# A mixture-of-experts stage with rows in blocks of 256 and W1 as the stationary operand

## The chip, the cores and the metric

The kernel runs on one core of one Trainium2 chip. The metric is the device time of one execution in microseconds, from the median of several runs. One execution was also taken by the profiler; all rows of the profile come from that one.

## The reference, cut to what matters

A graph layer over 3125 nodes of 256 features: a message-passing part over 50,000 edges, a linear attention, and then the part that the change touches, a mixture of 8 experts with the two best experts per node:

```
logits = xt @ Wr + br                      # xt: 3125 x 256, 8 experts
top_p, top_idx = top_k(softmax(logits), 2)
weights = top_p / top_p.sum(-1)
xe = xn * ln_g[e] + ln_b[e]                # per expert
h  = gelu(xe @ W1[e] + b1[e])              # 256 -> 1024
y  = h @ W2[e] + b2[e]                     # 1024 -> 256
out = x + sum over the two experts of weight * y
```

3125 nodes x 2 choices make 6250 rows. The reference's own routing of its inputs gives the eight experts 949, 684, 740, 736, 734, 917, 618 and 872 rows.

## The kernel before, in words

The edge part runs from the start to about 585 us, two dense layers and a batch norm follow, then the routing builds lists of rows by expert (about 660 to 696 us). Meanwhile each expert's weights have been split once into a high part (rounded to the matmul's fp32r format) and a low part (the rest) and stored in a table in memory, `split_table`, of 4 MB per expert. A product is made of three matmuls: high x high, high x low, low x high.

The expert stage works on slots of 128 rows, all of one expert (`SLOTS` = 56; `MAIN` = 52 always run, the other 4 only if the lists need them). For slot j the steps are:

- POOL `fetch(j)` (L750): copies a column of row numbers (L752) and gathers 128 token rows from the token table with an indirect DMA (L757).
- PE `slot_transpose` (L1065) turns them; DVE `slot_scale` (L1759) applies ln_g and ln_b; ACT `slot_high` (L1355) and DVE `slot_low` (L1782) make the two parts.
- PE `slot_up` (L1080): 12 matmuls with the tokens stationary and 512 columns of W1 moving; the result has rows on partitions. DVE `slot_bias` (L1768) adds b1, broadcast over partitions, ACT `slot_gelu` (L1341) follows.
- PE `slot_hidden_transpose` (L1090): 8 transposes of 128x128; ACT `slot_copy` (L1348) and DVE `slot_copy` (L1775) take the high and low parts out of PSUM.
- PE `slot_down` (L1104): 24 matmuls of 256 columns. DVE `slot_out` (L1789) adds b2 into `ys`, ACT `slot_weigh` (L1359) multiplies by the gate weight.
- POOL `put(j)` (L761): copies the row numbers (L764) and adds the 128 rows to the output with an indirect accumulating DMA (L768). Before it copies the next row numbers it waits until the put before has landed (`acc_in`).

PE's order is written out by hand: `slot_step(j)` is hidden transposes of j, up of j+1, token transposes of j+2, down of j. A hardware loop of four steps reads the expert numbers into registers at its head (`experts_of`). POOL's order is fetch(j+4), put(j), fetch(j+5), put(j+1) and so on. `tok` holds 4 slots, `ys` 4 slots.

The weights of an expert are in `wsplit`, two sets by the parity of e. SP waits until `y_b` says that all slots of expert e-2 are through, loads the two biases (L547, L548) and the 4 MB of expert e (L544), and announces them with `w_ready`. With the lists of these inputs this happens inside the stage for e = 2 to 7; the loads of experts 0 and 1 come before it.

## Time and profile before

| | |
|---|---|
| median of 3 runs (lowest, highest) | 1082.4 us (1082.07, 1085.88) |
| the profiled execution | 1084.07 us, its span 1082.2 us |
| PE busy over the span | 973.2 us, 90% |
| DVE, ACT, POOL busy | 628.0, 507.3, 574.0 us |
| expert stage, from the row lists to the end | 696 to 1082 us |
| mean granted TensorE clock | 0.971 of full speed |

The span is the time from the first to the last instruction; the execution's own time has 1.9 us around it. Busy time of PE is that of pipelined matmuls, so it counts overlaps of neighbours once. A line such as L1104 is a line of the kernel; the same line can stand for PE (the matmul) and PEld (the load of its stationary operand). "Idle before" an instruction is followed by what ended it; "issue" means that nothing which the profile shows was waited for.

### The profile page before, as it was taken

The page shows a single profiled execution, that of the slowest core. Times are in us where ns is not written, and L with a number is a line of the kernel's source. Part 1 is how long each engine was busy: PE and PEld are TensorE (multiplying, and loading weights), DVE is VectorE, ACT ScalarE, POOL GpSimd, SP SyncE. Part 2 cuts the span into 40 slices and gives each one's busy share as a digit, 9 for nine tenths or more (in the row PEclk, how much of TensorE's full clock was granted, in tenths as well). Part 3 has the DMA queues.
Part 4 walks back from the last instruction along what each step waited for, and adds up shares of the span by engine and source line. Part 5 has one row for each costly group of instructions (what it writes and reads, how often), then busy time and mean ns, then how long its engine had stood idle before and what let it go on. Part 6 is the DMA issues. An engine that isn't in the chain of part 4 may idle for free.

```text
span 1082.2 us, 18882 instructions
## 1 busy us (share of the span) xinstructions
PE 973.2 (90%) x5439; PEld 819.6 (76%) x5440; DVE 628.0 (58%) x1185; ACT 507.3 (47%) x1030; POOL 574.0 (53%) x632
## 2 busy tenths in 40 slices
PE   3898899999999999799998971599999999999995
PEld 2587788888878878687785551588888888888894
DVE  6555455555545555488884158655555555555552
ACT  3654455545445454355543445434444444444442
POOL 3377777777777777767770030124253353453442
PEclk9999999999999999899999986899999999999998
DMA  9767778787777877997752019412545626635321
GB/s 228 214 147 242 249 246 262 237 279 236 251 253 238 269 248 248 280 301 240 248 183 84 25 48 330 185 30 35 201 79 180 212 49 205 189 69 149 103 34 21
DMA packets 98047, 198.29 MB, mean 183 GB/s; under 512 B 19875, under 2 KB 52843, under 8 KB 96954
## 3 DMA queue, kind: packets, MB, share of 16 engines
q1 hardware_dynamic: 67358, 131.60, 35.1%
q0 software_dynamic: 28896, 64.46, 24.5%
q10 hardware_dynamic: 1724, 1.42, 0.6%
q8 instruction: 31, 0.51, 0.2%
q14 instruction: 38, 0.31, 0.1%
HBM read 147.86 MB, written 49.97 MB: 183 GB/s over the span
## 4 chain that ended last, share of the span: by engine, by line
PE 64%; POOL 14%; DVE 7%; issue 7%; DMA 5%; ACT 1%; SPq 0%; DVEq 0%; POOLq 0%; ACTq 0%
POOL work L715 14%; PE banks L1104 13%; PE banks L1080 13%; PE banks L451 10%; PE banks L439 9%; PE banks L1090 4%; PE banks L428 2%; PE banks L979 2%; PE banks L989 2%; PE banks L918 2%; DMA work<-node_table,srcT 2%; PE banks L863 2%; DMA work<-token_table,tokc 1%; DMA xs<-in_x 1%; PE banks L1065 1%
## 5 line engine op out<-in xcount | busy, mean ns | idle before, releaser
L715 POOL DMA_INDIRECT work<-node_table,srcT x396 | 397.4, 1003 | 160.1 <-issue 117.7
L487 DVE TENSOR_TENSOR work<-banks,work 128x512 f32<-128x512 f32 x198 | 128.9, 682 | 117.4 <-DMA work<-node_table,srcT 114.4
L451 PE MATMUL banks<-work 128*128 128x256 f32 x792 | 186.5, 386 | 9.1 <-issue 8.5
L439 PE MATMUL banks<-w_edge,eaT 128*128 128x256 f32 x792 | 182.9, 380 | 3.0 <-DVE work L487 3.0
L451 PEld LDWEIGHTS banks<-work 128*128 128x128 f32 x792 | 152.0, 193 | 33.8 <-issue 13.0
L439 PEld LDWEIGHTS banks<-w_edge,eaT 128*128 128x128 f32 x792 | 144.9, 190 | 21.5 <-DVE work L487 4.6
L1104 PE MATMUL banks<-wsplit,hidT_hi 128*128 x832 | 155.9, 288 | 1.7 <-DVE hidT_lo L1775 1.7
L1080 PE MATMUL banks<-wsplit,xeT_hi 128*128 x416 | 134.8, 405 | 2.7 <-DVE xeT_lo L1782 2.7
L475 ACT ACTIVATE work<-work 128x512 f32<-128x512 f32 x198 | 113.7, 626 | 39.9 <-DVE work L487 39.9
L768 POOL DMA_INDIRECT out<-work,rowc x52 | 83.7, 1609 | 90.3 <-ACT work L1359 59.6
L1104 PEld LDWEIGHTS banks<-wsplit,hidT_hi 128*128 128x128 f32 x832 | 129.2, 191 | 2.1 <-issue 1.9
L464 ACT COPY wts<-banks 128x256 f32<-128x256 f32 x66 | 24.6, 373 | 217.4 <-PE banks L451 217.4
L1104 PE MATMUL banks<-wsplit,hidT_lo 128*128 x416 | 117.7, 283 | 0.0
L1341 ACT ACTIVATE work<-work 128x512 f32<-128x512 f32 x104 | 65.7, 632 | 101.6 <-DVE work L1768 101.6
L1775 DVE TENSOR_TENSOR hidT_lo<-banks,hidT_hi 128x512 fp32r<-128x512 f32 x104 | 67.0, 686 | 63.6 <-ACT hidT_hi L1348 63.5
L1080 PEld LDWEIGHTS banks<-wsplit,xeT_hi 128*128 128x128 f32 x416 | 75.1, 191 | 16.8 <-issue 3.4
L1768 DVE TENSOR_TENSOR work<-banks,wts 128x512 f32<-128x512 f32 x104 | 71.5, 688 | 21.4 <-PE banks L1080 19.9
L1080 PE MATMUL banks<-wsplit,xeT_lo 128*128 x208 | 82.3, 396 | 0.0
L1104 PEld LDWEIGHTS banks<-wsplit,hidT_lo 128*128 128x128 f32 x416 | 79.6, 191 | 0.0
L757 POOL DMA_INDIRECT work<-token_table,tokc x52 | 52.6, 1012 | 45.9 <-POOL tokc L752 40.7
L1359 ACT ACTIVATE work<-work,slot_f 128x256 f32<-128x256 f32 x52 | 26.5, 509 | 100.7 <-DVE work L1789 100.7
L1090 PE MATMUL banks<-ident,work 128*128 128x128 f32 x416 | 54.7, 274 | 10.9 <-issue 10.0
(226 smaller groups left out, 1414.5 us busy)
## 6 DMA issues: line engine op xcount, KB each, us to landing
wsplit<-split_table SPq DMA_DIRECT2D x8, 4096.0 KB, 14.7
work<-in_edge_attr SPq DMA_DIRECT2D x65, 384.0 KB
wts<-in_L_ffn_W SPq DMA_DIRECT2D x64, 256.0 KB, 5.0
split_table<-raw_hi SPq DMA_DIRECT2D x64, 256.0 KB, 2.6
split_table<-raw_lo SPq DMA_DIRECT2D x64, 256.0 KB, 4.4
work<-node_table,srcT POOLq DMA_INDIRECT x396, 5.1
xs<-in_x SPq DMA_DIRECT2D x8, 560.0 KB
wts<-in_L_ffn_b SPq DMA_DIRECT2D x8, 512.0 KB, 3.8
```

The source lines that it names most:

```text
L439: last = nc.tensor.matmul(b[:, k * DIM:(k + 1) * DIM], eaT[:, u, 2 * q + k], w_edge[:], start=True, stop=True)
L451: last = nc.tensor.matmul(bank[5][:, 0:DIM], onehot[:, u, j], msg[:, u, j], start=(j == 0), stop=(j == GT - 1))
L475: nc.scalar.activation(msg[:, u, 2 * q:2 * q + 2], msg[:, u, 2 * q:2 * q + 2], ACT.Relu).then_inc(msg_ready, 1)
L487: nc.vector.tensor_tensor(msg[:, u, 2 * q:2 * q + 2], bank[2 + q][:].rearrange("p (k c) -> p k c", k=2), xg[b][:, 2 * q:2 * q + 2], ALU.ad ...
L715: pool.indirect_dma_start(out=xg[n % NB][0:rows, j], out_offset=None, in_=node_table, in_offset=bass.IndirectOffsetOnAxis(ap=srcT[0:rows, ...
L768: pool.indirect_dma_start(out=out, out_offset=bass.IndirectOffsetOnAxis(ap=rowc[:, u:u + 1], axis=0), in_=ys[:, b], in_offset=None, bounds ...
L1080: last = nc.tensor.matmul(bank[1 + c][:], x[:, u, k], w, start=(k == 0 and m == 0), stop=(k == 1 and m == 2))
L1090: last = nc.tensor.transpose(bank[3 + c][:, k * P:(k + 1) * P], hid[:, u, (4 * c + k) * P:(4 * c + k + 1) * P], ident[:])
L1104: last = nc.tensor.matmul(bank[5][:, 0:DIM], x[:, k], w_set[:, lo:lo + DIM], start=(k == 0 and m == 0), stop=(k == HIDDEN // P - 1 and m = ...
L1341: nc.scalar.activation(s, s, ACT.Gelu).then_inc(hid_g, 1)
L1768: nc.vector.tensor_tensor(hid[:, u, c * 512:(c + 1) * 512], bank[1 + c][:], b1, ALU.add).then_inc(hid_b, 1)
L1775: nc.vector.tensor_tensor(hidT_lo[:, 4 * c:4 * c + 4], bank[3 + c][:].rearrange("p (k c) -> p k c", k=4), hidT_hi[:, 4 * c:4 * c + 4].bitc ...
```

## The change

The expert stage works on blocks of 256 rows of one expert (`BLOCKS` = 32, `MAIN` = 28 always run). The diff, cut to its core:

```
+ROWS = 2 * P
+BLOCKS = (2 * NODES + EXPERTS * (ROWS - 1)) // ROWS
+SLOTS = 2 * BLOCKS
-MAIN = SLOTS - 4
+MAIN = BLOCKS - 4
...
+        w1_hi = nc.alloc_sbuf_tensor_at("w1_hi", [P, HALVES, HIDDEN], F32R, ...)
+        w1_lo = nc.alloc_sbuf_tensor_at("w1_lo", [P, HALVES, HIDDEN], F32R, ...)
...
         def load_biases(sp, e):
-            sp.dma_start(bias[:, e % 2, 0:HIDDEN], a["L0_ffn_b1"][e].partition_broadcast(P))...
-            sp.dma_start(bias[:, e % 2, HIDDEN:HIDDEN + DIM], a["L0_ffn_b2"][e].partition_broadcast(P))...
+            sp.dma_start(bias[:, e % 2], a["L0_ffn_b2"][e].partition_broadcast(P))...
```

PE: W1 is the stationary operand, so the hidden rows come out transposed already; the hidden transposes go away.

```
+            def up(i, u, fresh):
+                pe.wait_ge(xeT_low, i + 1)
+                for m in range(MS):                       # MS = 8 pieces of 128 hidden columns
+                    if m % 2 == 0:
+                        pe.wait_ge(w1_high, MS // 2 * i + m // 2 + 1)
+                        pe.wait_ge(w1_low, MS // 2 * i + m // 2 + 1)
+                        if not fresh:
+                            pe.wait_ge(hid_g, MS * (i - 1) + m + 2)
+                    for k in range(HALVES):
+                        for n, (x, w) in enumerate(((xeT_hi, w1_hi), (xeT_lo, w1_hi), (xeT_hi, w1_lo))):
+                            last = nc.tensor.matmul(bank[1 + m // 2][:, m % 2 * ROWS:(m % 2 + 1) * ROWS],
+                                                    w[:, k, m * P:(m + 1) * P], x[:, u, k], ...)
+                    if m % 2 == 1:
+                        last.then_inc(hid_ps, 1)
...
+            def down(i, u, e, fresh):
+                for m in range(2):
+                    if not fresh:
+                        pe.wait_ge(y_b, 2 * i + m - 1)
+                    for k in range(MS):                   # 24 matmuls of 256 columns into bank 5 + m
...
+            def block_step(i, u, tu, r, e_here, fresh=False):
+                up(i + 1, 1 - u, False)
+                turn(i + 2, tu, r, False)                 # 4 token transposes
+                down(i, u, e_here, fresh)
```

ACT: bias and gelu in one instruction, straight out of PSUM, and the low part of W1 copied to its fixed buffer. `b1T` is filled once, by a transpose and a copy before the stage.

```
+            def block_gelu(i, u, e, e_next, fresh):
+                for b in range(MS // 2):
+                    act.wait_ge(hid_ps, MS // 2 * i + b + 1)
...
+                    for m in (2 * b, 2 * b + 1):
+                        nc.scalar.activation(hid[:, m], bank[1 + b][:, ...], ACT.Gelu,
+                                             bias=b1T[:, bass.ds(e, 1), m]).then_inc(hid_g, 1)
+                    act.wait_ge(hid_g, MS * i + 2 * b + 2)
+                    nc.scalar.copy(hidT_hi[:, u, 2 * b:2 * b + 2], hid[:, 2 * b:2 * b + 2])...
+                    if e_next is not None:
+                        weights_low(i + 1, b, e_next, False)
```

`weights_low` (ACT) and `weights_high` (DVE) copy one of four pieces, 128x512, of the low and high W1 of block i's expert from `wsplit` to `w1_lo` and `w1_hi`; at the first piece they wait for `w_ready`, and for each piece until `up` of the block before has read it. DVE's order in the loop for block i is, for b = 0 to 3, `weights_high(i + 2, b)` and `hidden_low(i + 1, b)` (with `block_scale(i + 2)` before the last pair), then `block_low(i + 2)` and `block_out(i)` for both halves.

POOL: a block is fetched and put in two halves of 128 rows, as pairs.

```
+            def fetch(i, r, u, fresh):
+                pool.wait_ge(tok_in[u], 32 * r)
+                if not fresh:
+                    pool.wait_ge(tok_T, i - TOKS + 1)
+                for m in range(2):
+                    nc.gpsimd.tensor_copy(tokc[...], tok_i[:, bass.ds(2 * i + m, 1)]).then_inc(cur_ready, 1)
+                    pool.wait_ge(cur_ready, 2 * i + m + 1)
+                    pool.indirect_dma_start(out=tok[:, 2 * u + m], ...).then_inc(tok_in[u], 16)
+            def put(i, u, fresh=False):
+                for m in range(2):
+                    if not fresh or m == 1:
+                        pool.wait_ge(acc_in, 16 * (2 * i + m))
+                    nc.gpsimd.tensor_copy(rowc[:, m:m + 1], row_i[:, bass.ds(2 * i + m, 1)]).then_inc(row_ready, 1)
+                    pool.wait_ge(row_ready, 2 * i + m + 1)
+                    pool.wait_ge(y_w, 2 * i + m + 1)
+                    pool.indirect_dma_start(out=out, ..., in_=ys[:, 2 * u + m], compute_op=ALU.add).then_inc(acc_in, 16)
...
+            fetch(AHEAD, 0, AHEAD, True)                  # AHEAD = 3; blocks 0 to 2 are fetched before
+            put(0, 0, True)
+            with pool.Fori(0, (MAIN - 4) // TOKS) as t:
+                for k in range(TOKS):
+                    fetch(TOKS * (t + 1) + k, t + 1, k, False)
+                    put(TOKS * t + 1 + k, (1 + k) % 2)
```

`tok` holds 4 blocks, `ys` 2 blocks (4 halves); `hidT_hi` and `hidT_lo` are doubled. The routing rounds each expert's rows up to 256 instead of 128.

## Rows read from the trace of the kernel before

**Rows 1.** The page's first line.
```profile
span 1082.2 us, 18882 instructions
```

**Rows 2.** Windows: stretch, its us, busy PE, PEld, DVE, ACT, POOL, clock, DMA share, GB/s.
```profile
699.00:715.00 16.00, 11.91 (x56) 9.54 (x57) 7.14 (x15) 4.71 (x9) 4.61 (x8) 0.79 0.12 34
715.00:765.00 50.00, 48.86 (x336) 44.60 (x335) 29.14 (x58) 22.09 (x42) 21.12 (x28) 1.00 0.23 38
...
990.80:1060.00 69.20, 67.80 (x463) 61.77 (x462) 40.89 (x80) 31.63 (x60) 27.93 (x36) 1.00 0.38 103
```

**Rows 3.** Timeline of PE: one slot, and the head of the next loop.
```profile
848.85 1.04 PE L1090 MATMUL banks<-ident,work 128*128 128x128 f32 x8
849.64 0.70 PE L1080 MATMUL banks<-wsplit,xeT_hi 128*128 x2
...
852.62 0.48 PE L1104 MATMUL banks<-wsplit,hidT_hi 128*128 x2
...
856.47 1.09 PE L1090 MATMUL banks<-ident,work 128*128 128x128 f32 x8 [0.73 <-issue]
```

**Rows 4.** Timeline of POOL: two first fetches, put then fetch, fetch then put.
```profile
696.68 1.03 POOL L757 DMA_INDIRECT work<-token_table,tokc  x1 [0.83 <-POOL tokc L752]
...
698.71 1.00 POOL L757 DMA_INDIRECT work<-token_table,tokc  x1 [0.80 <-POOL tokc L752]
...
830.31 1.61 POOL L768 DMA_INDIRECT out<-work,rowc  x1 [0.93 <-POOL rowc L764]
...
833.00 1.01 POOL L757 DMA_INDIRECT work<-token_table,tokc  x1 [0.88 <-PE banks L1065]
...
870.35 1.01 POOL L757 DMA_INDIRECT work<-token_table,tokc  x1 [0.89 <-POOL tokc L752]
...
872.50 1.61 POOL L768 DMA_INDIRECT out<-work,rowc  x1 [0.94 <-POOL rowc L764]
```

**Rows 5.** Timeline of SP and POOL at the first and last of six loads.
```profile
766.04 0.43 SPq L544 DMA_DIRECT2D wsplit<-split_table  x1
...
766.68 1.61 POOL L768 DMA_INDIRECT out<-work,rowc  x1 [2.60 <-ACT work L1359]
...
781.98 0.18 POOL L764 COPY rowc<-row_i 128x1 int32 x1 [11.58 <-DMA out<-work,rowc]
783.10 1.61 POOL L768 DMA_INDIRECT out<-work,rowc  x1 [0.94 <-POOL rowc L764]
...
991.62 0.43 SPq L544 DMA_DIRECT2D wsplit<-split_table  x1
...
1006.66 0.18 POOL L764 COPY rowc<-row_i 128x1 int32 x1 [10.67 <-DMA out<-work,rowc]
```

**Rows 6.** Issue to landing of a put (L768), a fetch (L757), a load (L544).
```profile
DMA to landing us min/median/max: 3.7/3.8/15.3
...
DMA to landing us min/median/max: 2.7/2.8/12.7
...
DMA to landing us min/median/max: 13.4/14.7/15.8
```

**Rows 7.** Waits of PE in the stage: total us, times, longest.
```profile
PE banks L1065 <- DMA work<-token_table,tokc: 5.6, 2, 4.9
```

**Rows 8.** Chain that ended last, in time: first up, first down; the last put.
```profile
702.32 4.73 PE banks L1080 x12
...
713.03 2.87 PE banks L1104 x24
...
1073.54 1.57 POOL L768 DMA_INDIRECT out<-work,rowc  x1 [1.73 <-ACT work L1359]
```

**Rows 9.** Groups by line: busy us, mean ns, idle before.
```profile
L1274 ACT ACTIVATE work<-banks,cvec 128x448 f32<-128x448 f32 x14 | 8.9, 634 | 14.8 <-PE banks L979 14.8
...
L534 ACT CAST raw_hi<-wts 128x512 fp32r<-128x512 f32 x64 | 38.7, 604 | 0.0
...
L1775 DVE TENSOR_TENSOR hidT_lo<-banks,hidT_hi 128x512 fp32r<-128x512 f32 x104 | 67.0, 686 | 63.6 <-ACT hidT_hi L1348 63.5
```

More of the change, by code:

```diff
@@ L1058, in _, with turn @@
             pe.wait_ge(lists_ready, 1)
[L1060 to L1061 removed]
+            def turn(i, tu, r, fresh):
+                pe.wait_ge(tok_in[tu], 32 * (r + 1))
                 if not fresh:
[L1063 to L1066 removed]
@@ L1791, in slots, with weights_high @@
-            def slots(j0, n):
-                fresh, end, e = j0 == 0, j0 + n, {}
-                def experts(j, m):
-                    e.update(zip(range(j, j + m), experts_of(DVE, j, m)))
-                experts(j0, 3)
+            def weights_high(i, b, e, fresh):
+                if b == 0:
+                    dve.wait_ge(w_ready, e + 1)
+                if not fresh:
+                    dve.wait_ge(hid_ps, MS // 2 * (i - 1) + b + 1)
+                piece = slice(2 * b * P, 2 * (b + 1) * P)
+                w_set = wsplit[:, bass.ds(e % 2, 1), 0:HALVES * HIDDEN].rearrange("p a (k c) -> p (a k) c", k=HALVES)
+                nc.vector.tensor_copy(w1_hi[:, :, piece], w_set[:, :, piece].bitcast(F32)).then_inc(w1_high, 1)
@@ L1815, in _ @@
-            slots(0, MAIN)
+                        for b in range(MS // 2):
+                            weights_high(i0 + 1, b, e[i0 + 1], False)
+                            hidden_low(i0, 0, b)
+                for i in range(i0, end):
+                    u = (i - i0) % 2
+                    for b in range(MS // 2):
+                        if b == MS // 2 - 1 and i + 2 < end:
+                            block_scale(i + 2, u, e[i + 2], False)
+                        if i + 2 < end:
+                            weights_high(i + 2, b, e[i + 2], False)
+                        if i + 1 < end:
+                            hidden_low(i + 1, 1 - u, b)
+                    if i + 2 < end:
+                        block_low(i + 2, u, False)
+                    block_out(i, u, e[i])
+                    if u == 0 and i + 3 < end:
+                        experts(i + 3, min(2, end - i - 3))
```

376 lines of the change are left out of this document (166 added, 210 removed).

## The prediction

> **What bounds the kernel now.** I read the page first, then the trace by stretches. The span is 1082.2 us [rows 1]; the profiled execution took 1084.07, the median of the runs is 1082.4, so I count on the span and carry its end over almost one to one (0.2 us). The change touches only the expert stage, from the token lists at 696 us to the end, 386 us. There PE is busy for nearly the whole of each stretch at full clock, DVE and ACT for about half [rows 2]. One slot of PE [rows 3]: 8 hidden transposes in 0.79 us (848.85 to 849.64), up with 2 token transposes in 2.98 (to 852.62; up alone some 2.85), down of 24 matmuls in 2.87, 0.120 each [rows 8]. With the change-overs 6.73 us a slot, and each loop of four begins late by 0.93 us (down ends at 855.5, the next transposes start at 856.47). 52 slots x 6.73 + 12 x 0.93 = 361 us: PE sets the time, and little else is idle on its path.
>
> But POOL is not far behind, and this decides the case. A put costs: issue, landing 3.8 us later [rows 6], then the row copy and the next issue after 1.12 (a row copy at 781.98, the put at 783.10 [rows 5]), so 4.9 to 5.1 us between puts against 6.73 a slot. When SP loads an expert's 4 MB, the put issued some 0.65 us later lands only with the load's end: load 766.04, put 766.68, next row copy 781.98 after 11.58 us of idle; at the last, load 991.62, row copy 1006.66 [rows 5]. That is so in all six such loads (15.9, 15.1, 15.9, 16.2, 14.6, 15.0 us from load to row copy; mean 15.45), and the maxima of put and fetch landing, 15.3 and 12.7 us, say the same [rows 6]. POOL loses about 11.3 us each time and wins it back in the 6 to 8 slots that follow, because a slot leaves it 1.6 us. PE noticed it once, by 0.7 us (of the two waits for tokens, 5.6 us, the other 4.9 is the start) [rows 7].
>
> **The change, part by part.** The router gives 949, 684, 740, 736, 734, 917, 618 and 872 rows: 52 slots of 128 now, 27 blocks of 256 then. MAIN is 28, so 28 blocks run, one of them empty: 56 slots' worth of down and token transposes where there were 52.
>
> *PE per block.* Up becomes 48 matmuls of 256 columns with a 128-column weight load each, the shape and pitch of down, 0.120 us: 5.76 (two slots' up now: 5.7). Down: 48 x 0.120 = 5.76. Four token transposes: 0.45. Hidden transposes: none (2 x 0.79 saved). 12.0 us a block, against 13.46 for two slots.
>
> *Start.* Two fetches instead of one before the first transposes: +2.03 [rows 4]. Scale, high and low double in width: up(0) starts at 705.2 instead of 702.3 [rows 8]. Up(0) lasted 4.73 [rows 8] against 2.85, since PE came out of idle (the granted clock is 0.79 in that stretch, part of it at 1.2 GHz, and 1.00 afterwards [rows 2]): +1.9, so it ends at 712.9. Up(1) needs xeT_low(1), which DVE and ACT reach only after four gelu pieces of about 1.92 us behind the first hid_ps (707.9): 715.7, plus scale 1.0, high 0.6, low 0.7: 718.3. Again 1.9 for the clock after the idle: up(1) ends 726.0, down(0) ends 732.2. (Before, down(0) ended at 715.9.)
>
> *PE alone to the end.* 26 x 12.0 + 5.76 for the last down + 7 loop heads x 0.93 = 324.3: 1056.5. The last put: the final two downs are 5.76 apart but four puts are a chain of 4.92 each, so the last issue is at about 1064.8 and the end 8.66 later, as now (1073.54 to 1082.2) [rows 8]: 1073.4. So even with all else hidden the gain is 8.8 us.
>
> *ACT.* Per piece of 512: two gelus with a bias pointer (at most 0.634, the row for 448 columns out of PSUM; about 0.48 each by width), one copy to hidT_hi and one to w1_lo at 0.604 [rows 9]. Without any overlap 2.2, with the 0.1 by which neighbours overlap 1.92; four pieces 7.7 to 8.9, then high 0.6 and DVE's low 0.69. From the start of up(i+1) to xeT_low(i+2): 1.6 + 7.7..8.9 + 1.3 = 10.6 to 11.8, below the 12.0 of PE. Hidden, by 0.2 to 1.4 us; if that cover were gone, each 0.1 over in a piece would cost 0.4 x 28 = 11 us.
>
> *DVE.* Four w1_hi copies, four hidden lows, two scales, one low, two outs: 13 operations of at most 0.69 [rows 9] = 9.0 of 12. Hidden. The removed bias adds and the b1 DMA of 512 KB lay off the path: nothing. The extra small constant load, b1's transpose and its copy: under 0.5 us, once.
>
> *The fixed W1 buffer.* Its copies need w_ready one step before up does. A load lands 14.7 (13.4 to 15.8) us after issue [rows 6]; SP issues it about 0.45 after y_b. After three-block experts w_ready comes 2.3 us after DVE first wants it (at 0.9 after ACT does), within the slack above: 0 us, up to 2 x 5 = 10 at worst where POOL does not hide it. Behind DVE's wait stand the hidden lows of block i+1, which down wants some 9 us later, and behind ACT's the next gelu. SP's queue is one DMA shorter per expert (0.4 us, counted in the 0.45).
>
> *POOL.* This is the term that I put the prediction on. fetch(i+3) and put(i) are now pairs: the put of m=1 waits for the landing of m=0 with no fetch in between to use the time. A block costs POOL, from the put of m=0: 3.8 landing + 1.12; to the first fetch 2.69 (830.31 to 833.00); second fetch 2.12 (2.03 at the start, 696.68 to 698.71, plus some 0.1 for register addresses); row copy and issue 2.14 (870.35 to 872.50) [rows 4]: 11.9 us. Two slots cost it 10.2. PE's mean is 12.0 + 0.93/4 = 12.2. POOL now keeps pace, but wins back only 0.3 us a block where it loses about 8 at each load, three blocks apart. Six loads happen, after blocks 3, 6, 9, 12, 15 and 19. Who waits for POOL: fetch(i+4) lies behind put(i), and turn(i+4) stands on PE in front of down(i+2). With no lag its tokens are there 12.5 us after put(i,0), 6 us before PE asks. That is all the slack.
>
> I worked the sequence, block by block: D(i), end of down(i), is the later of D(i-1) + 12.0 (+ 0.93) and tokens(i+2) + 6.3; put(i,0) is the later of POOL's chain and D(i) - 0.7; a DMA in flight during a load lands 15.45 after the load's issue at D(i) + 1.1. The intervals put(i,0) to put(i+1,0) at the six loads come out as 18.4, 20.2, 17.1, 19.7, 23.1 and 20.0, thus 6.5, 8.3, 5.2, 7.8, 11.2 and 8.1 over 11.9: 47.1. PE stalls 10.8 (block 7), 0.5, 9.9 (13), 6.6 (17) and 10.8 (20). Sum over POOL: first put 731.5; 24 x 11.87 = 284.9; three last blocks without fetches 29.5; last pair 4.9; end 8.7; holds 47.1; idle waiting for PE's results 5.4: **1112**.
>
> Two bounds of it. Whether a put issued 1.8 us before the load is held too no row shows (all six were issued after it). Held: 1126. Not held, which I take: 1112. The Trainium skill (DMA: Bandwidth & Descriptors, Queues, rings and completion order) says that a completion increment lands only after every earlier write of that DMA engine, across queues; the long landings of the trace (15.3 against 3.8) agree, and by that rule a put ahead of the load isn't held, which would be the 1112. And the chain of 11.9 rests on pitches of single fetches; with 0.05 us more at each of four steps the same sequence gives 1120, with 0.4 us less a block 1099.
>
> **Rivals.**
> 1. *POOL stays hidden; PE sets the end.* 1073.6 us, by the sum above. For it: nearly all POOL waits of today cost PE nothing. Against it: a hold of 11.3 us must fit into 6 us of slack that refills at 0.3 a block. It decides if the hold falls below some 1 us a load, or if fetches run 2 us a block faster.
> 2. *POOL is slowed further by the new copies.* DVE's four w1_hi copies are the first SBUF to SBUF copies of the stage beside POOL's issues of 1.01 and 1.61 us [rows 4, 5]. If two of the four issues of a block each wait 0.3 us (a copy lasts at most 0.69), a block costs 0.6 more than 11.9; POOL then is slower than PE at every block, not just at loads: 1059.6 + 47 + 24 x 0.6 + 5 = about 1126; range 1120 to 1140. No row shows such a wait, since no such copy is there now. The Trainium skill (SBUF — State Buffer, Two separate sides, the "DVE blocks DMA" trap) states that a fp32 SBUF to SBUF tensor_copy on DVE shuts GpSimd out of descriptor writing while it runs, which speaks against this change and would give this rival's time; no run here shows it yet.
> 3. *In between:* holds of 2 to 5 us at a load, since the load now starts in another phase of POOL's loop, and slack for the first: 1080 to 1095.
> 4. *ACT or the early w_ready sets the pace* (piece over 2.3 us): +11 to +22 on 1073.6, 1085 to 1096, hidden where POOL is slower still.
>
> **How the numbers follow.** Forecast, POOL's chain with its holds (1095 to 1120): 0.50. Rival 2 with the held put (1120 to 1145): 0.18. Rival 1: 0.20. Rivals 3 and 4: 0.12. The likeliest is 1112; its own range is 1099 to 1126. Both signs hold much of the chance, so the range runs from 1074 (half of rival 1 left out) to 1134. What a measurement tells from no change is 0.5%, 5.4 us (the three runs spread over 3.8). Faster than 1077: 0.19; within 1077 to 1087.8: 0.07; slower: 0.74.
>
> **What would show it.** Right: per-block PE work of 12.0 us with up and down at 0.120 a matmul; PE idle of 5 to 11 us at token transposes, put down to the DMA of tok, after most of the six loads; POOL's idle time at rowc on the landing of puts grown; PE's busy share down although its work fell. Rival 1: PE gaps only at loop heads, last down near 1056. Rival 2: tokc copies or DMA_INDIRECT spans on POOL longer than 0.78, 1.01 and 1.61, ending with DVE copies. Wrong would be: up at another pitch than 0.120, or POOL's block much off 11.9.

## The result, and the profile after

The changed kernel takes 1133.85 us (median of 4 runs, 1132.44 to 1138.32) against 1084.14 (4 runs, 1082.07 to 1085.88): a ratio of 1.048, 95% interval 1.0457 to 1.0503. It is slower, by 49.7 us; the forecast of 1112 us lay 29.6 above the 1082.4 that it started from. Its profiled execution took 1134.73 us, span 1133.0.

The page's first line and its line of busy times:
```profile
span 1133.0 us, 19323 instructions
PE 970.8 (86%) x5848; PEld 845.7 (75%) x5849; DVE 598.0 (53%) x1134; ACT 600.9 (53%) x1251; POOL 598.9 (53%) x648
```

The windows, with the columns of [rows 2]: a stretch from just after one load to the end of the next, one without a load, 18 us around the start of a load (issued at 864.63), the first 17 us of the last load (issued at 1015.34), and, last, 8 us in which PE works again behind the first load's wait:
```profile
790.00:835.00 45.00, 31.18 (x225) 30.98 (x226) 17.44 (x34) 23.93 (x50) 18.58 (x24) 0.81 0.44 130
835.00:862.00 27.00, 26.51 (x220) 26.12 (x219) 12.44 (x25) 17.48 (x37) 13.42 (x17) 1.00 0.22 36
862.00:880.00 18.00, 8.00 (x63) 7.61 (x63) 5.13 (x10) 9.36 (x20) 5.93 (x7) 0.86 0.77 269
1015.00:1032.00 17.00, 6.67 (x51) 6.48 (x50) 3.35 (x7) 8.12 (x17) 4.55 (x5) 0.80 0.84 285
797.00:805.00 8.00, 7.35 (x41) 7.35 (x42) 2.96 (x6) 1.13 (x2) 3.71 (x4) 0.61 0.15 17
```
Without a load PE is busy for 98% of the stretch, at full clock, as in [rows 2]. While a load moves its bytes (DMA share 0.77 and 0.84) PE is busy for 8.0 of 18 and 6.7 of 17 us, and ACT and DVE, which work on its results, have gaps too.

Who waits for whom (us in total, times, longest):
```profile
POOL rowc L773 <- DMA out<-work,rowc: 124.2, 31, 13.4
PE banks L1077 <- DMA work<-token_table,tokc: 52.6, 8, 10.3
DVE work L1774 <- PE banks L1077: 42.1, 7, 9.7
```
PE's line is that of [rows 7], grown from 5.6 us to 52.6; 45.5 us of it, in 7 waits, lie behind the start. Six of the seven are long (5.3 to 10.3 us), one for each load, as the prediction said. POOL's wait for landings of puts has grown from 85.7 us (47 times, longest 11.8) in the kernel before to 124.2. PE's token transposes wait for tokens, and DVE for PE. DVE's W1 copies wait for the signal that the weights are there once, for 4.2 us.

The timeline of SP and POOL at the first of the six loads, to be read beside [rows 5]:
```profile
772.47 0.43 SPq L552 DMA_DIRECT2D wsplit<-split_table  x1
...
773.26 1.63 POOL L777 DMA_INDIRECT out<-work,rowc  x1 [0.93 <-ACT work L1367]
788.32 0.37 POOL L773 COPY rowc<-row_i 128x1 int32 x1 [13.43 <-DMA out<-work,rowc]
789.62 1.69 POOL L777 DMA_INDIRECT out<-work,rowc  x1 [0.93 <-POOL rowc L773]
790.72 1.03 POOL L762 COPY tokc<-tok_i 128x1 int32 x1
792.59 1.04 POOL L765 DMA_INDIRECT work<-token_table,tokc  x1 [0.84 <-POOL tokc L762]
```
The first put of the block is issued 0.79 us behind the load, and the row copy that waits for its landing starts 15.85 us after the load's issue. Only then can POOL put the other half and fetch the next tokens (792.59). PE finds them missing soon after. The chain that ended last goes through the same place at each load. From 749 us, shortly behind the start, to the last load it stays on POOL and its DMAs; only behind that load (from 1030.55) does it run over PE to the end. Three of its pieces (start, us, what), and a down and an up for comparison:
```profile
728.98 5.77 PE banks L1107 x48
...
822.23 12.37 DMA out<-work,rowc
...
855.90 3.89 DMA out<-work,rowc
868.95 12.17 DMA out<-work,rowc
...
1064.32 5.76 PE banks L1091 x48
```
A put lands in 3.9 us without a load (855.90) and holds the chain for 12.2 to 14.9 us with one (at the last load it is a fetch, 12.7 us). In the page's shares of the chain, landings of puts are 11% of the span.

### The profile page after: what moved, and what is told of

It is laid out like the page before. It is cut to its first block, busy times and chain, and to the rows that moved or that the text cites. A ratio compares the mean times of both kernels' runs of the same rounds, so it can differ in the third digit from the quotient of the medians.

```text
span 1133.0 us, 19323 instructions
## 1 busy us (share of the span) xinstructions
PE 970.8 (86%) x5848; PEld 845.7 (75%) x5849; DVE 598.0 (53%) x1134; ACT 600.9 (53%) x1251; POOL 598.9 (53%) x648
## 3 DMA queue, kind: packets, MB, share of 16 engines
q0 software_dynamic: 29664, 64.98, 23.6%
## 4 chain that ended last, share of the span: by engine, by line
PE 34%; POOL 24%; DMA 16%; issue 14%; DVE 7%; ACT 3%; POOLq 1%; ACTq 1%; DVEq 0%; SPq 0%
POOL work L722 17%; DMA out<-work,rowc 11%; PE banks L459 7%; PE banks L447 6%; PE banks L1107 4%; PE banks L1091 4%; POOL work L765 3%; DMA work<-node_table,srcT 3%; PE banks L987 2%; PE banks L997 2%; PE banks L926 2%; PE banks L436 2%; POOL out L777 2%; DMA work<-token_table,tokc 1%; POOL tokc L762 1%
## 5 line engine op out<-in xcount | busy, mean ns | idle before, releaser
L1107 PEld LDWEIGHTS banks<-wsplit,hidT_hi 128*128 128x128 f32 x896 | 149.5, 205 | 0.0
L483 ACT ACTIVATE work<-work 128x512 f32<-128x512 f32 x198 | 115.2, 627 | 57.1 <-DVE work L495 56.7
L1091 PE MATMUL banks<-xeT_hi,w_hi 128*128 128x256 f32 x448 | 129.8, 290 | 11.3 <-DVE xeT_lo L1781 10.3
L1091 PE MATMUL banks<-xeT_lo,w_hi 128*128 128x256 f32 x448 | 128.3, 286 | 0.0
L1091 PE MATMUL banks<-xeT_hi,w_lo 128*128 128x256 f32 x448 | 128.2, 286 | 0.0
L1796 DVE TENSOR_TENSOR hidT_lo<-work,hidT_hi 128x512 fp32r<-128x512 f32 x112 | 77.8, 694 | 86.1 <-ACT hidT_hi L1353 86.0
L1350 ACT ACTIVATE work<-banks,b1T 128x256 f32<-128x256 f32 x224 | 93.5, 468 | 34.2 <-PE banks L1091 34.2
L1091 PEld LDWEIGHTS banks<-xeT_hi,w_hi 128*128 128x128 f32 x448 | 87.6, 195 | 13.8 <-DVE xeT_lo L1781 8.6
L1091 PEld LDWEIGHTS banks<-xeT_lo,w_hi 128*128 128x128 f32 x448 | 87.6, 196 | 0.0
L1091 PEld LDWEIGHTS banks<-xeT_hi,w_lo 128*128 128x128 f32 x448 | 87.5, 195 | 0.0
## 6 DMA issues: line engine op xcount, KB each, us to landing
wsplit<-split_table SPq DMA_DIRECT2D x8, 4096.0 KB, 15.2
```

The source lines that it names most:

```text
L483: nc.scalar.activation(msg[:, u, 2 * q:2 * q + 2], msg[:, u, 2 * q:2 * q + 2], ACT.Relu).then_inc(msg_ready, 1)
L1091: last = nc.tensor.matmul(bank[1 + m // 2][:, m % 2 * ROWS:(m % 2 + 1) * ROWS], w[:, k, m * P:(m + 1) * P], x[:, u, k], start=(k == 0 and ...
L1107: last = nc.tensor.matmul(bank[5 + m][:, 0:DIM], x[:, u, k, m * P:(m + 1) * P], w_set[:, lo:lo + DIM], start=(k == 0 and n == 0), stop=(k ...
L1350: nc.scalar.activation(hid[:, m], bank[1 + b][:, m % 2 * ROWS:(m % 2 + 1) * ROWS], ACT.Gelu, bias=b1T[:, bass.ds(e, 1), m]).then_inc(hid_g, 1)
L1796: nc.vector.tensor_tensor(hidT_lo[:, u, 2 * b:2 * b + 2], hid[:, 2 * b:2 * b + 2], hidT_hi[:, u, 2 * b:2 * b + 2].bitcast(F32), ALU.subtra ...
```

## The experiments

Lengths are compared over the expert stage: from the first copy of token numbers on POOL to the end of the span. It is 386.6 us before (the copy ahead of the first fetch of [rows 4] is at 695.6) and 435.4 in the changed kernel (697.6 to 1133.0). The reason for this measure: on the chip that ran all but the last three experiments, the part ahead of the stage took 100 to 130 us longer in every kernel, e7's version of the kernel before included. A control, e12, is the changed kernel on that chip: its stage is 438.6 us. So e1 to e11 are to be read against 438.6 as much as against 435.4. Each stage length comes from one profiled execution. "Interval" is from the first put of a block to the first put of the next; PE's waits for tokens are those behind the start.

**First group: the fetch order, the loads, the new DVE work.**

*e1: the tokens fetched one block earlier.*
```
-            for k in range(AHEAD):          # AHEAD = 3
+            for k in range(TOKS):           # TOKS = 4
                 fetch(k, 0, k, True)
...
-                    put(TOKS * t + 1 + k, (1 + k) % 2)
+                    put(TOKS * t + k, k % 2)
```


> The changed kernel with one thing else: POOL's order is fetch(i+4), put(i) instead of fetch(i+3), put(i); pairs stay pairs. My theory (PE waits for tokens because fetches stand behind puts that a weight load holds): the tokens come one block, 12 us, earlier, so the slack before PE waits grows from 6 to 18 us. The waits of PE for tokens fall from 52.6 us to under 15, the profile's span from 1133 to 1085 to 1100. Rival A (the copies of W1 and the low parts slow everything by taking ports, the order of POOL's work does not matter): 1125 to 1135. Rival B (POOL's throughput alone is the bound, whatever the order): no more than 12 us saved, 1118 to 1125.

Measured: stage 444.2 us, longer than the changed kernel's on either chip. PE's waits for tokens fell only to 36.4 us, and a new wait stands beside them. Waits of e1, and DVE at one load (issued 988.34):
```profile
DVE work L1807 <- POOL rowc L773: 63.3, 11, 7.0
PE banks L1078 <- DMA work<-token_table,tokc: 36.4, 5, 8.6
```
```profile
988.25 1.63 POOL L777 DMA_INDIRECT out<-work,rowc  x1 [0.94 <-ACT work L1368]
1004.04 0.18 POOL L773 COPY rowc<-row_i 128x1 int32 x1 [14.16 <-DMA out<-work,rowc]
...
1011.20 0.42 DVE L1807 TENSOR_TENSOR work<-banks,wts 128x256 f32<-128x256 f32 x1 [6.33 <-POOL rowc L773]
```
The theory missed, and so did both rivals. In the changed kernel POOL lags at five of the six loads: the put that is held starts 1.9 to 5.0 us behind the load's issue, at four of them behind one or two fetches, and that time isn't idle. In e1 both fetches are issued ahead of every load and the held put starts with it (at five of six loads within 0.1 us): POOL idles 13.2 to 14.2 us each time instead of 10.4 to 13.4, and the interval at a load rose from 21.4 us (mean) to 22.8 to 24.9. PE runs on for a while on its reserve of tokens, until all four results (two blocks) wait for their puts and DVE can't empty PE's banks. The reserve only moves PE's wait; POOL's throughput is the limit, at 12.3 us a block with nothing to win back.

*e2: the same, and POOL's order in a block is fetch, put, fetch, put.*
```
+                    for m in range(2):
+                        fetch(TOKS * (t + 1) + k, t + 1, k, False, (m,))
+                        put(TOKS * t + k, k % 2, False, (m,))
```


> As the run before, and the halves interleaved: fetch(i+4, half 0), put(i, half 0), fetch(i+4, half 1), put(i, half 1), so that a fetch again fills the landing time of a put. My theory: POOL needs some 10.9 us a block instead of 12.6, below PE's 12.2, and recovers from each hold before the next: PE-bound, span 1074 to 1082, waits of PE for tokens under 8 us. Rival A (ports): 1120 to 1135. Rival B (POOL's throughput alone): 24 x 1.7 = 41 us saved, 1092.

Measured: stage 402.3 us, 33.1 less than the changed kernel (36.3 less than e12); PE's waits for tokens 21.2 us in 5. Each single fetch now fills the landing of a put. POOL can take a block in some 10.6 us (the shortest intervals) and wins back a part of what a load costs; at the loads the intervals are still 18.6 to 22.7, and the theory's PE-bound stage is not reached.

*e3: small loads from the third expert on.*
```
-            sp.dma_start(wsplit[:, e % 2].bitcast(F32), split_table[e])
+            sp.dma_start(wsplit[:, e % 2, 0:64].bitcast(F32), split_table[e, :, 0:64])     # e >= 2
```


> The changed kernel, its POOL order untouched, but the weight loads of experts 2 to 7 bring 64 columns (32 KB) instead of 8192 (4 MB); those experts compute with the weights of experts 0 and 1. My theory (holds during loads are the main loss; the six intervals with a load are 8.8 us longer than the others): no holds, span 1078 to 1088. If the paired chain of 12.6 us a block were the loss and not the holds: 1110 to 1125. If ports were: 1120 to 1133.

Measured: stage 384.6 us, 50.8 less than the changed kernel and 54.0 less than e12, on the same chip. PE's waits for tokens are 3.6 us in 2, the longest of POOL's waits for a landing is 4.0 us, and the intervals between the start and the last blocks are 12.0 to 13.6. This edit leaves POOL's order alone and takes only the bytes away, so it is the load's traffic that costs these 51 to 54 us.

*e4: DVE's W1 copies reduced to 2 of 256 columns.*
```
-                piece = slice(2 * b * P, 2 * (b + 1) * P)
+                piece = slice(2 * b * P, 2 * b * P + 2)      # all but the first block
```


> The changed kernel, but from the second block on DVE copies 2 columns of each W1 high piece instead of 256 (the high part of W1 stays that of expert 0 in all other columns). My theory gives these copies (0.42 us each) a share of the 0.7 us by which POOL's block is longer than forecast: POOL issues next to them are stretched by up to 0.4 us, 0.1 to 0.3 us a block, so span 1123 to 1131. The rival that they take POOL's port for most of the loss: 1110 or less. If they cost nothing: 1132 to 1134.

Measured: stage 435.5 us, as in the changed kernel and 3.1 under e12; POOL's intervals without a load are 12.54 us, in e12 12.68. So the copies cost 0 to 3 us: the rival is out, and the theory's small share can't be told from nothing.

*e5: DVE's subtraction for the hidden low part reduced to 2 of 256 rows.*
```
-                nc.vector.tensor_tensor(hidT_lo[:, u, 2 * b:2 * b + 2], hid[:, 2 * b:2 * b + 2], ...
+                n = ROWS if i < 2 else 2
+                nc.vector.tensor_tensor(hidT_lo[:, u, 2 * b:2 * b + 2, 0:n], hid[:, 2 * b:2 * b + 2, 0:n], ...
```


> The changed kernel, but from the third block on DVE's subtraction for hidT_lo works on 2 of 256 rows (the low part of the hidden rows is left out). It is the stage's one frequent DVE instruction that reads two SBUF tensors, 0.69 us; before the change its like read PSUM. In the trace after, 10 of the 12 row copies of POOL that last 0.37 to 0.72 us instead of 0.19 lie over such an instruction, 9 of these end within 0.05 us of it. Theory (POOL's copies are held by it): row copies back to 0.19 and the expert stage (from the first copy of token numbers to the end, 435.4 us in the changed kernel) 4 to 10 us shorter, 425 to 431. Rival (coincidence): copies stay as long and the stage is 434 to 436. Only stages are compared, as the edge part on another chip may take another time.

Measured: stage 437.4 us, no gain (1.2 under e12). The reason for trying it was in the changed kernel's timelines of POOL and DVE:
```profile
1011.38 0.71 POOL L773 COPY rowc<-row_i 128x1 int32 x1 [2.41 <-DMA out<-work,rowc]
...
1011.36 0.69 DVE L1796 TENSOR_TENSOR hidT_lo<-work,hidT_hi 128x512 fp32r<-128x512 f32 x1
```
A row copy of POOL that usually lasts 0.19 us lasts 0.71 and ends with DVE's subtraction. In the changed kernel 12 of the 56 row copies last over 0.3 us, 4.0 us more in all; with the small subtraction 7 of them, 1.6 us more. The wait is real, but 2.4 us of it, spread over 28 blocks, didn't show in the stage.

The subtraction isn't the only holder, and row copies aren't all that is held. Of the 12 long row copies 3 end with a W1 copy, of e5's 7 it is 5; that of 788.32 above ends 0.04 us behind one. Puts stretch as well: one that starts while DVE is in a subtraction or a W1 copy lasts until 1.5 us after the end of that instruction.
```profile
788.22 0.43 DVE L1790 CAST w_hi<-wsplit 128x512 fp32r x1 [4.23 <-SPq L664]
...
948.41 0.42 DVE L1790 CAST w_hi<-wsplit 128x512 fp32r x1
948.46 1.87 POOL L777 DMA_INDIRECT out<-work,rowc  x1 [0.93 <-POOL rowc L773]
```
12 of the 56 puts last over 1.7 us instead of 1.6, 3 of them by a W1 copy; in the kernel before it is 1 of 52, and in e4, with the W1 copies small, 8, none by a W1 copy. All of it together is some 8 us of POOL's time in the changed kernel. No run takes both DVE instructions away.

**Second group: what a load in parts does.**

*e6: the load in eight parts of 512 KB, two on their way at a time.*
```
+            for q in range(PARTS):                                   # 8
+                s, base = ((w_in[e % 2], 0), (x_in[e % 2], 32))[q % 2]
+                if q >= 2:
+                    sp.wait_ge(s, base + 16 * (PARTS // 2 * (e // 2) + q // 2))
+                sp.dma_start(wsplit[:, e % 2, q * n:(q + 1) * n].bitcast(F32), ...).then_inc(s, 16)
```


> The changed kernel, each expert's 4 MB loaded by eight DMAs of 512 KB of which never more than two are under way. Theory (a put or fetch lands only after all that was queued before it in the DMA engines): a hold is at most about 1 MB of transfer, 3 to 4 us instead of 9 to 15, but two or three puts and fetches meet the load; the stage goes from 435.4 to 400 to 415 us. Rival (a put waits until no load is under way at all): stage 430 to 440, the longest wait of the row copy still 12 to 14 us. Second rival (SP's waits stretch the load so that the W1 copies come late): row copy waits short, but PE waits on w1_high or xeT_lo, stage over 415.

Measured: stage 416.9 us, so the second rival was right. The longest hold fell from 13.4 to 6.7 us, PE's waits for tokens to 11.5 in 9. But the load now takes longer (its parts are issued over 16.8 us), and its signal comes too late for the W1 copies, for which the fixed buffer makes DVE and ACT ask a step before PE does. Waits of e6:
```profile
POOL rowc L781 <- DMA out<-work,rowc: 100.9, 34, 6.7
DVE w_hi L1798 <- SPq L672: 43.1, 5, 10.4
PE banks L1099 <- DVE xeT_lo L1789: 28.1, 9, 6.0
```

*e7: the same edit of the load on the kernel before.*

> The kernel before with the same loads in parts. It lets POOL win back each hold already, so theory: 0 to 1 us, ratio 0.998 to 1.001, the longest wait of POOL's row copy down from 11.8 to under 5 us. If the holds cost the old kernel time that the waits don't show: ratio below 0.995.

Measured: ratio 1.0046 (1.0001 to 1.0092), stage 386.1 us against 386.6. The longest wait of POOL for a landing is 4.5 us instead of 11.8, and that buys nothing (the time is, if anything, 0.5% longer): the kernel before had the holds too, and POOL won them back.

*e8: e2 and e6 together.*

> The changed kernel with fetches one block earlier, halves interleaved and loads in parts. Theory: POOL needs 10.6 us a block (measured with the interleaved order), wins back 1.6 a block and meets no hold over 4 us: PE sets the time with 12.2 us a block; stage 377 to 386 us, ratio to the kernel before 0.990 to 0.999. Rival (lower throughput of POOL still bounds it): stage 390 to 400, ratio 1.003 to 1.012.

Measured: ratio 1.0315 (1.027 to 1.0361), stage 421.7 us, longer than e2's 402.3 and above both forecasts. Behind the start PE never waits for tokens. What PE waits for is the weights' signal, through DVE and ACT:
```profile
DVE w_hi L1802 <- SPq L672: 55.3, 5, 11.5
ACT w_lo L1354 <- SPq L672: 37.5, 5, 8.7
```
The cure of the one wait became the other: with no hold left, five of the six loads stop the copies of W1, up to 11.5 us each.

**Third group: the order alone, the floor, W1 first, and a control.**

*e9: the interleaved order without the earlier fetch.*
```
-                    fetch(TOKS * (t + 1) + k, t + 1, k, False)
-                    put(TOKS * t + 1 + k, (1 + k) % 2)
+                    for m in range(2):
+                        fetch(TOKS * (t + 1) + k, t + 1, k, False, (m,))
+                        put(TOKS * t + 1 + k, (1 + k) % 2, False, (m,))
```


> POOL's order in a block goes from fetch, fetch, put, put to fetch, put, fetch, put; the tokens are fetched at the same block as in the changed kernel, so this is one half of the edit that gave a stage of 402.3 us (the changed kernel: 435.4). Theory (the two fetches, 4.2 us, then stand behind the landings of the puts instead of between them and the next one, so POOL's block falls from 12.6 us to about 10.6, and the held landing costs as before): intervals of 10.6 to 12.2 us without a load, since PE's 12.0 now sets them; stage 400 to 412 us. Rival (the fetch one block earlier did it, by giving PE more in reserve against each hold): the intervals stay at 12.5 and the stage at 425 to 435.

Measured: stage 449.1 us, the longest of all; both sides missed. PE's waits for tokens are 57.1 us in 13, and they occur at blocks without a load too (intervals 13.2 to 15.6). POOL between two loads, and POOL's two largest waits:
```profile
958.88 1.60 POOL L778 DMA_INDIRECT out<-work,rowc  x1 [3.27 <-ACT work L1369]
...
961.52 1.18 POOL L766 DMA_INDIRECT work<-token_table,tokc  x1 [0.84 <-POOL tokc L763]
```
```profile
POOL out L778 <- ACT work L1369: 101.6, 28, 21.4
POOL rowc L774 <- DMA out<-work,rowc: 74.9, 20, 11.8
```
POOL waits 3.27 us for the result of the block's first half before it may put it, and the fetch of the second half stands behind. With tokens only three blocks ahead, PE then waits for POOL's fetch and POOL for PE's result, in turn.

*e10: interleaved order, earlier fetch, small loads.*

> The interleaved order with the earlier fetch, and from the third expert on only 64 of each partition's 8192 columns of weights are loaded (the rest of the wide copy keeps the weights of the expert before; all else is done as before). It puts the holds and POOL's block aside together and shows what PE alone would give. Theory (PE is then the bound, 12.0 us a block, 32 blocks): stage 374 to 380 us, below the 384.6 of the run with small loads alone and below the 386.6 of the kernel before. Rival (a block costs more than PE's matmuls even without holds and with POOL at 10.6 us: DVE or ACT, or POOL's own throughput): stage at or above 384.

Measured: stage 376.0 us, no wait of PE for tokens behind the start. This is what PE alone gives; 28 blocks ran, not the 32 that the expectation names. The window between start and tail, at full clock, busy for 98%:
```profile
855.00:1150.00 295.00, 290.27 (x2408) 288.09 (x2407) 157.69 (x315) 221.08 (x461) 161.50 (x188) 1.00 0.26 44
```

*e11: interleaved order, earlier fetch, and W1's parts of the load first, with their own signal.*
```
+                c = (0, 1, 4, 5, 2, 3, 6, 7)[q]            # W1 high, W1 low, W2 high, W2 low
...
+                    sp.wait_ge(w1_high, done * 2)           # the last copies of W1 of expert e - 2
+                    sp.wait_ge(w1_low, done * 2)
+                load_weights(sp, e, 0)
+                weights_there(e, 0)                         # w_ready = 2e + 1: DVE and ACT may copy W1
                 sp.wait_ge(y_b, done)
                 load_biases(sp, e)
+                load_weights(sp, e, 1)
+                weights_there(e, 1)                         # w_ready = 2e + 2: PE may start down
```


> The interleaved order with the earlier fetch, and each load in eight parts of 512 KB, two on their way at a time: first the four of W1, which start when the last copies of W1 of the expert two before are made (about a block before its last result), and which have their own signal; then, after that expert's last result, the four of W2, for which PE waits at the second layer. Theory (holds of the put's landing by whole loads cost about 50 us, and once the loads are in parts what is left is that the signal for W1 comes late, 57.0 us of waits in the run with all three edits): both gone, no wait of DVE for the weights above 3 us, longest wait of POOL for a put's landing under 7 us, stage 376 to 386 us, so the whole is 0.99 to 1.00 of the kernel before. Rival (the time that the bytes take on the queues lands on the puts however they are cut): stage above 395 us, ratio above 1.01.

Measured: stage 378.6 us, ratio 0.9975 (0.9922 to 1.0028). Of the waits for the weights' signal two are left, 2.5 us together; the longest wait for a landing is 4.5 us. The first put came 39.6 us into the stage, in e10 37.2.

*e12: the changed kernel once more, on the chip of the experiments so far.*

> The changed kernel itself on this chip, where the part before the experts takes longer. Theory and rivals agree, if the stage can be compared between chips: stage 433 to 438 us, the four last intervals with a load 20 to 23.6 us. If it is off by more than 4 us, the stage lengths of the other runs have to be read against this one instead.

Measured: stage 438.6 us, 3.2 more than on the first chip. Differences of 3 us between stages say nothing; those used here are 8 us and more, or come with their intervals.

**Fourth group: the order and the loads taken apart.**

*e13: W1 first alone, POOL's queue as in the changed kernel.*

> The changed kernel with only its loads of weights changed: parts of 512 KB, two on their way, W1's first and on their own signal. POOL's queue is that of the changed kernel (fetch, fetch, put, put, tokens three blocks ahead). Theory (the whole loads carry nearly all of the loss, POOL's order only the 8.6 us between the runs with small loads, 384.6 and 376.0): stage 386 to 394 us, intervals without a load 12.5 us, PE's waits for tokens under 5 us in all. Rival (without the reserve of the earlier fetch every part that holds a put by 3 to 7 us reaches PE, as in the run with the load in parts alone, 416.9): stage 400 to 415.

Measured: stage 410.0 us; the rival was right. PE waits for tokens 18.6 us in 8, none of them over 4.1, and POOL for landings 95.5 us, none over 5.7. POOL can't win back even small holds in its paired order.

*e14: e11, with the parts of the first two experts issued without waits between them.*
```
-                if q >= 2:
+                if q >= 2 and e >= 2:
```


> The version of the last table (parts, W1 first, interleaved order, earlier fetch), with the parts of the first two experts issued without waits between them, so that SP is not held ahead of the stage and the second load is over when the first tokens are fetched. Theory: first put 37.2 us after the token lists instead of 39.6, stage 375 to 378 us, ratio to the kernel before 0.990 to 0.996. Rival (the first put came late for another reason): first put and stage as they were, 39.6 and 378.6.

Measured: 1072.91 us (6 runs, 1071.47 to 1074.87) against 1085.38 (11 runs) of the kernel before on that chip: ratio 0.9892 (0.9859 to 0.9925), stage 375.7 us, first put at +37.0. The theory held; this version is 1.1% faster than the kernel before. The window of the steady part, and SP and POOL at a load:
```profile
740.00:1050.00 310.00, 305.43 (x2533) 303.22 (x2532) 165.43 (x327) 230.56 (x481) 161.66 (x194) 1.00 0.49 124
```
```profile
807.74 17.92 SPq L558 DMA_DIRECT2D wsplit<-split_table  x8
...
807.38 1.74 POOL L796 DMA_INDIRECT out<-work,rowc  x1 [1.56 <-ACT work L1390]
...
815.53 0.25 POOL L792 COPY rowc<-row_i 128x1 int32 x1 [3.49 <-DMA out<-work,rowc]
816.72 1.60 POOL L796 DMA_INDIRECT out<-work,rowc  x1 [0.94 <-POOL rowc L792]
```
The hold that was 13.43 us of idle is 3.49 here, and 4.9 at most in the run. PE is busy for 98.5% of 310 us with all loads inside, at clock 1.00. (The view joins the four parts of W2 and the four of the next expert's W1 into one row of eight.) The chain that ended last is PE's own; the same down recurs every four blocks:
```profile
775.84 5.77 PE banks L1130 x48
...
825.02 5.77 PE banks L1130 x48
```

*e15: POOL's interleaved order alone, with small loads.*

> POOL's interleaved order without the earlier fetch, with the small loads. Theory (in this order each fetch stands behind a put that waits for a result of the same block, so with tokens only three blocks ahead POOL and PE wait for each other in turn, loads or not): PE waits for tokens also here, 5 us or more in all, stage 382 to 392 us. Rival (the order costs only where a load holds a put): no waits for tokens, stage 376 to 378 us as with the earlier fetch.

Measured: stage 394.9 us; PE waits for tokens 13.9 us in 12, none over 1.8. The theory's direction, beyond its upper end of 392. The circle between POOL and PE is there without any load.

The stages in one table (us; before: 386.6). 435.4 is from the run of the result; 410.0, 375.7 and 394.9 are from the chip of e13 to e15, all others from the chip of e12:

| loads of weights | as changed | fetch earlier | interleaved | both |
|---|---|---|---|---|
| whole, 4 MB | 435.4 (438.6) | 444.2 | 449.1 | 402.3 |
| in parts, one signal | 416.9 | not run | not run | 421.7 |
| in parts, W1 first | 410.0 | not run | not run | 378.6, 375.7 |
| small | 384.6 | not run | 394.9 | 376.0 |

## Why the prediction was too low

The mechanism was right; the term that failed first is *POOL's block*. It was put at 11.9 us, 0.3 below PE's 12.2, and measured 12.58, 0.3 above PE's 12.3. So the step "wins back only 0.3 us a block" failed: POOL won back nothing. The holds themselves were 5.6 us short in all, and the start 3.2.

The changed kernel's stage is 435.4 us. Read the table by differences: 376.0 is PE alone, 8.6 are POOL's paired order and late fetch without any load (384.6), 50.8 the whole loads on top (54.0 against e12). The kernel before pays 386.6. So the change did give PE 10.6 us, and gave 59.4 back.

The measured 1133.85 us lies above the band that was given to POOL's chain (1095 to 1120) and above the likeliest value's own range (to 1126). It lies inside rival 2's 1120 to 1140, but not by rival 2's cause, as shown below.

- **PE per block, 12.0 us: right.** Up 5.76, token transposes 0.44, down 5.77: 11.97. With the loop head, e14's chain has 49.18 us for four blocks (775.84 to 825.02), 12.3 a block; 12.2 was the forecast.
- **PE alone to the end, 1073.4: right.** Counted from the stage's start at 695.6 that is a stage of 377.8; e10 and e14 measured 376.0 and 375.7.
- **The start: 3.2 us short.** The first put came at 734.74 instead of 731.5. The stage itself began 2.0 us later than before, for which the prediction had no term (in e13 and e14, on another chip, it began at 695.8, as before, so the change need not be the cause); the remaining 1.2 are the start's own.
- **ACT and DVE hidden: right.** ACT's piece is 1.92 us (two neighbouring pieces start at 749.26 and 751.18), the lower of the two bounds.
- **w_ready hidden behind POOL: right as it stood, and what e6 and e8 uncovered.** One wait of 4.2 us in the changed kernel. The price named for a lost cover, 2 x 5 = 10 us, was for a whole load; with the load stretched by parts, e6 and e8 paid 43 and 55 us of waiting in it.
- **The holds: the mechanism right, the intervals too small by 9.9 us.** The six intervals at loads sum to 128.2 us; the forecast was 6 x 11.87 + 47.1 = 118.3. Of the 9.9, 4.3 are the longer block (6 x 0.71) and 5.6 the holds: 8.8 us a load beyond a block of 12.58, where the forecast had 7.85 beyond 11.87. They are more even (20.2 to 23.6) than the worked sequence (17.1 to 23.1).
- **POOL's block, 11.9 us: too small; this is the term that failed.** The 18 other intervals up to the last blocks sum to 228.0 us, where 18 x 11.87 and the 5.4 for waits on PE make 219.1: 8.9 us short. Seventeen of them, without the start's 14.2, average 12.58 (12.64 the eleven between the loads, where the chain is POOL's alone). Step by step, measured against forecast: from the first put to the second 5.38 against 4.92, on to the first fetch 2.78 against 2.69, to the second fetch 2.12 against 2.12, to the next block's put 2.30 against 2.14. So two thirds of the 0.71 lie between the two puts: the row copy starts 4.03 us after the put instead of 3.8, lasts 0.36 instead of 0.18, and the issue behind it waits 0.05 longer. The forecast took the landing alone for the first of these; in the kernel before the row copy, too, starts 3.8 to 4.2 us after a put (median 3.97). The long row copies are those that end with a DVE instruction, and the prediction took its steps from rows without such holds; its own note, 0.05 us more at each of four steps and 1120, went the right way and not far enough. Three issues of POOL wait 1.8 to 1.9 us instead of 0.84 to 0.94 with nothing in the profile to wait for, at 803.37, 839.44 and 1007.35, 2.8 us in all beyond that; only the first stands at a loop's end, so the heads of POOL's loop explain little.
- **The tail:** the last three blocks 29.6 us against 29.5; the last pair and the end 12.5 against 13.6.

The terms add up: 3.2 + 9.9 + 8.9 + 0.1 - 1.1 = 21.0, from 1112 to the span of 1133.0.

Put by cause, the 21.0 are 13.2 of POOL's block (4.3 + 8.9), 5.6 of the holds, 3.2 of the start and -1.0 of the end. The argument that "a hold of 11.3 us must fit into 6 us of slack that refills at 0.3 a block" was the right core, and it was still kind: the paired order refilled nothing (12.58 against PE's 12.3), so each load's loss went on to PE.

Of the two bounds, the put 1.8 us ahead of a load was taken as not held. The runs bear that out and show where it turns. In e9 and e2 five puts start 0.22 to 0.87 us ahead of a whole load, and the next row copy comes 15.3 to 16.0 us after them; four start 1.44 to 1.79 us ahead, and it comes 4.7 to 6.9 us after them instead of some 4: slowed, but not held to the load's end. Between 0.87 and 1.44 us no run has a put. A put's issue lasts 1.6 us. One of each kind, from e9 and from e2:
```profile
938.41 1.60 POOL L778 DMA_INDIRECT out<-work,rowc  x1 [1.73 <-ACT work L1369]
940.07 0.44 SPq L552 DMA_DIRECT2D wsplit<-split_table  x1
944.90 0.40 POOL L774 COPY rowc<-row_i 128x1 int32 x1 [2.64 <-DMA out<-work,rowc]
```
```profile
1118.86 1.60 POOL L778 DMA_INDIRECT out<-work,rowc  x1 [0.93 <-ACT work L1371]
1119.73 0.43 SPq L552 DMA_DIRECT2D wsplit<-split_table  x1
1134.77 0.18 POOL L774 COPY rowc<-row_i 128x1 int32 x1 [12.28 <-DMA out<-work,rowc]
```
In the changed kernel five of the six loads have a put 2.3 to 5.8 us ahead that isn't held, and the next block's first put, behind the load, is: at the load of 864.63 they are the puts of 861.59 and 868.95.
```profile
861.59 1.75 POOL L777 DMA_INDIRECT out<-work,rowc  x1 [0.93 <-POOL rowc L773]
...
867.54 0.47 POOL L773 COPY rowc<-row_i 128x1 int32 x1
868.95 1.63 POOL L777 DMA_INDIRECT out<-work,rowc  x1 [0.94 <-POOL rowc L773]
881.27 0.18 POOL L773 COPY rowc<-row_i 128x1 int32 x1 [10.69 <-DMA out<-work,rowc]
```
The Trainium skill (DMA: Bandwidth & Descriptors, Queues, rings and completion order) has a completion increment land only after every earlier write of its DMA engine; the puts of 861.59 and 868.95 agree with it.

Rival 2, POOL slowed by DVE's W1 copies, is right in its mechanism and wrong in its size. Its price was 0.6 us a block; without the copies (e4) a block is 0.14 us shorter than on the same chip with them, and the stage 3.1 us at most. W1 copies do hold POOL now and then: the put of 948.46 above, started 0.05 us into one, lasted 1.87 us. The Trainium skill (SBUF — State Buffer, the "DVE blocks DMA" trap) has GpSimd locked out while DVE runs such a copy; this put agrees. But only 3 of the 12 puts over 1.7 us are of this kind, and a put that starts before the copy, as that of 868.95, keeps its 1.63 us.

Rival 1's time was reached, but only with three edits that the change doesn't have (e14). Rival 4's mechanism set the pace only in e6 and e8.

What stays open: why the stage starts 2.0 us later; what the three long waits for an issue are; and what POOL's block would be with both kinds of DVE instruction out of its way. The split into steps is read from one trace; no run isolates it.

## What to carry to other kernels

An engine that is hidden by a margin must also win back every stall; before widening blocks, work out both its time per block and what it wins back per block after the longest stall. Fewer, larger steps on the bound engine can take the second away: here 1.6 us a slot became nothing. A long transfer beside short ones that are waited for one by one is worth cutting in parts, but then the consumer of the load must be given its first bytes on a signal of their own, and the fetches here were given both an earlier place and an order in which each fills another's landing; each of these edits alone leaves the stage longer than before (410.0 or 416.9 with the parts, 444.2, 449.1), and together they give 375.7, where the kernel before has 386.6. Whether cut loads with their own signal need both changes of the fetches or only one was not run.

## What the runs showed of the hardware that was not expected

- POOL's tiny row copies (0.19 us) stretch up to 0.72 us and end 0.04 us behind a DVE instruction that works from SBUF to SBUF: a subtraction with two SBUF inputs (0.69 us, 9 of 12 cases) or a W1 copy (0.42 us, 3 of 12). A put that starts within such an instruction lasts until 1.5 us after its end, up to 2.22 us instead of 1.6. It is common and cheap: e4 gained 3.1 us at most, e5 1.2.
- A put's landing behind a whole 4 MB load waits for nearly the whole load (13.43 us of idle), behind 512 KB parts, two on their way, 3.5 to 6.7 us. A put that starts 1.44 us ahead of the load isn't held, one that starts 0.87 us ahead is. A part lands 3.6 to 9.6 us (median 4.3, e14) after its issue; those over 6.1 are of the first two experts, issued without waits between them. The whole load lands after 13.8 to 16.4 us (median 15.2), so eight parts in pairs need 16.8 us of issuing (e6) where one load needed 15.2 in all.
- In the 16 us of the first load (772 to 788) PE works on and the granted clock is 1.00. Then PE waits 7.90 us for tokens, and in the 8 us in which it works again (797 to 805) the granted clock is 0.61, a part of it at 1.2 GHz: its down takes 7.97 us instead of 5.77. From 806 to 819 it is 1.00 again, 2.4 GHz. Behind each of the six waits the down is longer, by 1.2 to 2.3 us, but only the last of these downs (7.46 us) lies on the chain that ended last, which stays on POOL up to there.
